# Written-out first attention with row moments taken inside it, and a routing stage normalized on two engines

## The chip, the core and the metric

The program runs on one core of a Trainium2 chip. A core has five engines that work side by side, each through its own queue of instructions in order: PE (TensorE, matmul and transposes), DVE (VectorE), ACT (ScalarE), POOL (GpSimd) and SP (SyncE, which here only issues DMA). They are ordered among one another by semaphores alone. The metric is the device time of one execution in microseconds, as the median of several runs. Before the change it is 2719.99 us, the median of three runs (2716.86 to 2720.1).

## What is computed

Two layers over a graph of 2708 nodes with 256 features. Layer 0 is a graph attention with four heads, followed by a mixture of experts; layer 1 is a masked attention with four heads, followed by 30 steps of a small feed-forward network. The change touches the end of layer 0's attention and the start of its mixture of experts:

```python
x = x + _L0_gnn_ref(_layernorm(x, axis=-1), adj, ...)          # graph attention
x = x + _L0_ffn_ref((_layernorm(x, axis=-1))[None], ...)[0]    # mixture of experts

# in _L0_gnn_ref, for each head
logits = f1[:, None, :] + f2[:, :, None]
w = jax.nn.leaky_relu(logits, NEG_SLOPE)
masked = w * adj_mat
neg = jnp.where(adj_mat != 0.0, masked, -jnp.inf)
e = jnp.exp(neg - m); attn = e / denom
out = jnp.einsum('hnm,hmo->hno', attn, support)

# in _L0_ffn_ref: 16 experts, 2 chosen
gate_logits = x @ gate_w + gate_b
topk_vals, topk_idx = jax.lax.top_k(gate_logits, K)
topk_w = jax.nn.softmax(topk_vals, axis=-1)
```

The layer norm between the two needs the mean and the variance of every row of x after the attention. These are the "row moments" of the title.

## The kernel before, in words

The 2708 rows lie in 22 tiles of 128 partitions (the last tile overlaps the one before), taken as 11 pairs (`NPAIR`). x stays in `X` for the whole kernel. Every stage is a `Phase` with a block of instructions per engine and a barrier of all engines at its end (the line of the barrier is L55 or L58).

*Layer 0's attention* (`layer0_attention`, tiles named `a_`). The work is a sequence of 88 units, one for each tile and head. For a unit, PE makes the logits in three chunks (L717, L719), DVE adds and applies the leaky part per chunk (`leaky`, L626), multiplies by the mask with a running maximum (`mask`, L635) and negates the maximum (L638); ACT takes the exponential (L571); PE transposes the weights in 22 squares (`turn`, L732), ACT copies them out of PSUM (L526), and PE multiplies them by the values (`weighted`, 44 matmuls a unit, L747). After two heads ACT copies the sums, PE turns them back (L755) and DVE scales and adds them to X (`finish`, L658). The stages of a unit are spread over the steps of later units. `over_units` (L431) writes the order: the first pair and the last pair are written out, and the nine between are a loop of three rounds whose body holds three pairs, because the buffers go round by three (`LB`):

```python
    pair(0, 0)
    with eng.Fori(0, (NPAIR - 2) // LB) as m:
        for r in range(LB):
            pair(m * LB + (r + 1), r + 1)
    pair(NPAIR - 1, NPAIR - 1)
```

PE, DVE and ACT each run this loop. Some waits of ACT and DVE stand on a `nop` of their own. POOL prepares the mask tiles, and SP loads the adjacency rows.

*Routing* (`moe_route`, tiles named `m_`). DVE takes `bn_stats` of each of the 22 tiles (L142) and folds them into moments in four batches (`row_moments`, L94 to L101); POOL, after its constants, computes the inverse deviation of a batch (`inverse_deviation`, L108 to L113, with a power at L111) and normalizes tile by tile into `XF` (`standard_rows`, L118). PE transposes a tile (L1484), ACT copies it (L1540), PE multiplies by the gate (L1492) and DVE adds the bias into the logits (L1553). PE alternates between the transposes of one tile and the product of the tile before. Then follows a chain, mostly on DVE, that picks two experts for each row and sorts the rows by expert (L1570 to L1661). Meanwhile SP issues the loads of the gate (L1408 to L1410, the last being beta), 32 loads of expert weights, and at last the stores of XF; POOL adds beta to X (L1472).

*Experts* (`moe_experts`). POOL gathers the sorted rows tile by tile (L1705), PE transposes them (L1732) and multiplies (L1742, L1752); DVE stages the weights of a tile's expert (L1783), copies the transposed rows (L1785) and adds the second bias (L1793). SP loads two biases at the start (L1694, and 2 MB for the second, L1695). DVE waits for that second bias after it has staged two tiles and before it stages the third.

## Time and profile before

| | us |
|---|---|
| median of three runs | 2719.99 |
| the profiled execution | 2717.6 |
| its span | 2715.9 |
| mean granted clock of PE, share of full | 0.952 |
| busy: PE, DVE, ACT, POOL | 2481.9, 2011.5, 1614.1, 1426.9 |
| layer 0's attention in the timeline | about 74 to 773 |
| routing | 773.8 to 851.4 |
| experts, from the first gather | 853.1 |

A row of the timeline gives the start, the duration, the engine, the line of the kernel, the operation, what it writes and reads, how many in a row (xN), and in brackets how long the engine was idle before it and what released it. "issue" means that nothing which the profile shows was waited for. PEld is the loading of weights, which overlaps PE. An engine with a q at its end (POOLq) is its sequencer.

### The profile page before, as it was taken

The numbers are of one execution on the slowest core, as the hardware profiler recorded it, in microseconds if no ns is written. First come the engines' busy times: TensorE is split into PE (matmuls) and PEld (weight loads), VectorE is DVE, ScalarE is ACT, GpSimd is POOL, SyncE is SP. The second block draws the span as 40 slices with busy tenths as digits, with TensorE's granted clock in tenths as the row PEclk, the third lists the DMA queues.
The fourth block names the chain that finished last, engine by engine and source line by source line (L and its number), as shares of the span: only waits on it lengthen the run. The fifth ranks groups of instructions, "written<-read, shape, count | busy, mean of one in ns | idle before, by whom it ended". The sixth has DMA issues, their size and how long they took to land. (4 is left out here: it accounts for less than half of the span.)

```text
span 2715.9 us, 59651 instructions
## 1 busy us (share of the span) xinstructions
PE 2481.9 (91%) x20186; PEld 2029.7 (75%) x20187; DVE 2011.5 (74%) x4258; ACT 1614.1 (59%) x3050; POOL 1426.9 (53%) x1747
## 2 busy tenths in 40 slices
PE   6799999999975999097999999999689999999999
PEld 5377777777764998075777777777578888888888
DVE  5899989899945443787777777777667777777776
ACT  1577777777730332244666666666467777777775
POOL 6366666666451554432111122111388888888886
PEclk9799999999976999598999999999899999999999
DMA  2011111111054222301111111110000000000001
GB/s 99 21 43 49 56 43 43 43 63 43 22 197 148 70 72 62 126 16 35 55 41 41 41 41 41 45 58 21 7 1 0 0 0 0 0 0 0 0 0 41
DMA packets 43885, 114.26 MB, mean 42 GB/s; under 512 B 5621, under 2 KB 29918, under 8 KB 37982
## 3 DMA queue, kind: packets, MB, share of 16 engines
q1 hardware_dynamic: 38174, 97.16, 10.2%
q0 software_dynamic: 5568, 15.21, 1.8%
q8 instruction: 87, 1.43, 0.2%
q14 instruction: 56, 0.46, 0.1%
HBM read 99.21 MB, written 13.15 MB: 41 GB/s over the span
## 5 line engine op out<-in xcount | busy, mean ns | idle before, releaser
L2145 PE MATMUL f_pm<-f_wl,f_yt 128*128 128x256 f32 x2640 | 625.6, 380 | 0.0
L2145 PEld LDWEIGHTS f_pm<-f_wl,f_yt 128*128 128x128 f32 x2640 | 477.2, 191 | 51.6
L1089 POOL TENSOR_TENSOR ADJ<-ADJ,a_off 128x2708 f32<-128x2708 f32 x22 | 131.2, 5962 | 543.1 <-DVE ADJ L1168 543.1
L118 POOL TENSOR_SCALAR f_yy<-f_th,f_rs 128x255 f32<-128x255 f32 x660 | 367.5, 573 | 21.8 <-POOL f_rs L113 21.8
L526 ACT COPY a_wt<-a_tp 128x512 f32<-128x512 f32 x528 | 256.9, 566 | 155.3 <-PE a_tp L732 155.3
L1995 DVE SCALAR_TENSOR_TENSOR f_gg<-f_th,f_pm 128x512 f32<-128x512 f32 x319 | 219.0, 687 | 171.4 <-ACT f_th L2089 170.3
L549 POOL TENSOR_SCALAR a_off<-ADJ 128x677 bf16<-128x677 f32 x84 | 278.3, 3334 | 78.3 <-DMA ADJ<-in_adj 63.7
L626 DVE SCALAR_TENSOR_TENSOR a_lg<-a_f1s,F2S,a_fo 128x1024 f32<-128x1024 f32 (+1 forms) x264 | 294.5, 1152 | 30.8 <-issue 17.1
L1148 DVE CUSTOM_DVE_ANT_0 a_sc<-a_qk,ADJ 128x1024 f32<-128x1024 f32 (+1 forms) x264 | 288.3, 1093 | 30.4 <-PE a_qk L1246 30.4
L2089 ACT ACTIVATE f_th<-f_pm 128x512 f32<-128x512 f32 x319 | 190.5, 597 | 199.7 <-PE f_pm L2145 199.7
L1112 ACT ACTIVATE a_sc<-a_sc,a_mx 128x1024 f32<-128x1024 f32 (+1 forms) x264 | 277.7, 1052 | 45.3 <-DVE a_mx L1153 45.3
L1063 ACT COPY a_wt<-a_tp 128x512 f32<-128x512 f32 x264 | 154.2, 584 | 236.2 <-PE a_tp L1268 235.5
L635 DVE CUSTOM_DVE_ANT_0 a_lg<-a_lg,ADJ 128x2708 f32<-128x2708 f32 x88 | 262.0, 2977 | 7.4 <-issue 0.7
L1268 PE MATMUL a_tp<-ident,a_sc 128*128 128x128 f32 x1936 | 261.7, 276 | 0.2
L732 PE MATMUL a_tp<-ident,a_lg 128*128 128x128 f32 x1936 | 247.4, 277 | 6.6 <-issue 6.0
L1268 PEld LDWEIGHTS a_tp<-ident,a_sc 128*128 128x128 f32 x1936 | 215.5, 141 | 42.1 <-issue 19.4
L2002 DVE BATCH_NORM_STATS2 f_st<-f_th 128x6 f32<-128x256 f32 x660 | 245.8, 414 | 0.0
L1289 PE MATMUL a_po<-a_wt,V 128*64 128x128 f32 x3872 | 240.3, 276 | 0.0
L1289 PEld LDWEIGHTS a_po<-a_wt,V 128*64 128x64 f32 x3872 | 208.7, 137 | 41.5 <-issue 36.3
L1063 DVE COPY a_wt<-a_tp 128x512 f32<-128x512 f32 (+1 forms) x264 | 158.3, 599 | 107.9 <-PE a_tp L1268 107.9
L747 PEld LDWEIGHTS a_po<-a_wt,V 128*64 128x64 f32 x3872 | 209.6, 137 | 37.1 <-issue 35.1
L732 PEld LDWEIGHTS a_tp<-ident,a_lg 128*128 128x128 f32 x1936 | 211.0, 142 | 33.2 <-issue 21.4
(295 smaller groups left out, 4572.0 us busy)
## 6 DMA issues: line engine op xcount, KB each, us to landing
ADJ<-in_adj SPq DMA_DIRECT2D x44, 1354.0 KB, 5.8
W<-in_L_ffn_w SPq DMA_DIRECT2D x32, 512.0 KB, 9.8
m_got<-YD SPq DMA_DIRECT2D x6, 768.0 KB, 10.4
out<-X SPq DMA_DIRECT2D x21, 128.0 KB
X<-in_x SPq DMA_DIRECT2D x3, 768.0 KB, 9.9
XD<-XF SPq DMA_DIRECT2D x3, 768.0 KB
m_b<-in_L_ffn_b SPq DMA_DIRECT2D x1, 2048.0 KB, 8.4
m_rows<-XD,SLOT POOLq DMA_INDIRECT x58, 2.8
```

The source lines that it names most:

```text
L118: return eng.tensor_scalar(out, x, rs[:, 0, bass.ds(t, 1)], rs[:, 1, bass.ds(t, 1)], ALU.mult, ALU.add)
L526: copy(wt[:, h // 2, h % 2, j:end, :], tp[:, BANKS[g], 0:(end - j) * P]).then_inc(copied[BANKS[g]], 1)
L549: pool.tensor_scalar(off[:, b, cols], adj[:, b, cols], 0.0, HUGE, ALU.is_equal, ALU.mult).then_inc(off_done[b], 1)
L626: dve.scalar_tensor_tensor(lg[:, unit.turn, c0:c0 + cn], f1s[:, h, c0:c0 + cn], F2S[:, bass.ds(i * 2 + b, 1), h], fo[:, s, 0:cn], ALU.add, ...
L635: dve.tensor_tensor_reduce(lg[:, unit.turn, :], lg[:, unit.turn, :], adj[:, b, :], 1.0, FLOOR, ALU.mult, ALU.max, mx[:, h, 0:1]).then_inc( ...
L732: mm = pe.transpose(tp[:, BANKS[g], (j - j0) * P:(j - j0 + 1) * P], lg[:, unit.turn, col:col + P], ident[:, :])
L1063: copy(wt[:, (hp * NC + c) % 2, s, j - c * CT:end - c * CT, :], tp[:, bank(group), 0:(end - j) * P]).then_inc(copied[bank(group)], 1)
L1112: act.activation(sc[:, h, c0:c0 + cn], sc[:, h, c0:c0 + cn], ACT.Exp, bias=mx[:, h, NC:NC + 1], accum_out=den[:, h, c:c + 1]).then_inc(exp ...
L1148: dve.tensor_tensor_reduce(sc[:, h, c0:c0 + cn], qk[:, s, 0:cn], adj[:, b, c0:c0 + cn], 1.0, -BIG, ALU.add, ALU.max, mx[:, h, c:c + 1]).th ...
L1268: mm = pe.transpose(tp[:, bank(group), (j - j0) * P:(j - j0 + 1) * P], sc[:, h, col:col + P], ident[:, :])
L1289: mm = pe.matmul(po[s * HD:(s + 1) * HD, 0:P], V[:, j, 2 * hp + s, 0:HD], wt[:, (hp * NC + c) % 2, s, j - c * CT, :], start=(j == 0), stop ...
L2145: mm = pe.matmul(out, yt[:, g, r, k, :], wl[:, k, :], start=(k == 0), stop=(k == KD - 1))
```

## The change

It has six parts.

1. `over_units` writes all 11 pairs out; the loop and its registers are gone on PE, DVE and ACT. The nops of ACT and DVE before the waits in the attention are gone as well (one in `rows_of`, one in `leaky`, one in `mask`).
2. DVE takes the row statistics of tiles 0 to 20 inside the attention (`row_stats`), at head 3 of the following tile, folds them into moments behind the last step, and POOL computes the inverse deviations of these 21 columns at its end, into the tensor `GW`, which now lives from there on and is called `scales` in the routing.
3. In the routing only the last tile's statistics are left. DVE normalizes the odd tiles and POOL the even ones; POOL's constants come after.
4. PE transposes and multiplies two tiles at a time; ACT copies 512 columns at once, and DVE adds the bias to two tiles at once. DVE's and ACT's loops there are written out.
5. A small tensor, `slot`, now lies in the space of `xt`.
6. In the experts SP waits for the first two gathers before it issues the load of the second bias.

The core of the diff:

```diff
-def inverse_deviation(pool, mom, rs, neg_half, s0, s1, chain, base):
+def inverse_deviation(pool, mom, rs, neg_half, s0, s1, chain, base, out=None):
 
 
     n = slice(s0, s1)
+    out = rs if out is None else out
     pool.tensor_scalar(rs[:, 2, n], mom[:, 1, n], EPS, None, ALU.add).then_inc(chain, 1)
     pool.tensor_scalar(rs[:, 3, n], mom[:, 0, n], -0.5, None, ALU.mult).then_inc(chain, 1)
     pool.wait_ge(chain, base + 1)
-    pool.tensor_tensor(rs[:, 0, n], rs[:, 2, n], neg_half[:, n], ALU.pow).then_inc(chain, 1)
+    pool.tensor_tensor(out[:, 0, n], rs[:, 2, n], neg_half[:, n], ALU.pow).then_inc(chain, 1)
     pool.wait_ge(chain, base + 3)
-    return pool.tensor_tensor(rs[:, 1, n], rs[:, 3, n], rs[:, 0, n], ALU.mult)
+    return pool.tensor_tensor(out[:, 1, n], rs[:, 3, n], out[:, 0, n], ALU.mult)
...
         for b in range(2):
             for h in range(H):
                 step(Unit(i, b, h, number * 2 * H + b * H + h))
-    pair(0, 0)
-    with eng.Fori(0, (NPAIR - 2) // LB) as m:
-        for r in range(LB):
-            pair(m * LB + (r + 1), r + 1)
-    pair(NPAIR - 1, NPAIR - 1)
+    for i in range(NPAIR):
+        pair(i, i)
...
             with pool.Fori(1, NPAIR) as i:
                 for b in range(2):
                     tile(i, b)
+            pool.wait_ge(x_moments, 1)
+            inverse_deviation(pool, mom, rs, neg_half, 0, NT - 1, x_pchain, 0, scales)
...
-                act.nop(nofuse=True)
...
-                dve.nop(nofuse=True)
...
+            def row_stats(unit):
+
+                i, b, h0 = unit
+                dve.wait_ge(heads_out, pairs(unit))
+                dve.bn_stats(st[:, i * 2 + b, :], X[:, i * 2 + b, :]).then_inc(x_stats, 1)
...
                     finish(unit.later(-4))
+                if unit[2] == H - 1 and unit.later(-H - 1):
+                    row_stats(unit.later(-H - 1))
                 if ahead:
...
             over_units(dve, step)
+            dve.wait_ge(x_stats, NT - 1)
+            row_moments(dve, st, mom, 0, NT - 1, x_folded, 0).then_inc(x_moments, 1)
             finish(last_unit(0))
             finish(last_unit(H - 2))
...
             for k, (a, end) in enumerate(BATCHES):
                 s0, s1 = 2 * a, min(2 * end, NT - 1)
-                sp.wait_ge(xf_done, 2 * end)
+                sp.wait_ge(xf_even, end)
+                sp.wait_ge(xf_odd, end)
                 sp.dma_start(keep["XD"][1 + P * s0:1 + P * s1, :].rearrange("(t p) d -> p t d", p=P),
                              XF[:, s0:s1, :]).then_inc(stored, 16)
...
             pool.memset(zero[:, :], 0.0).then_inc(zero_ok, 1)
+            for t in range(0, NT, 2):
+                standard_rows(pool, XF[:, t:t + 1, :], X[:, t:t + 1, :], scales, t).then_inc(xf_even, 1)
+                if t == 0:
+                    pool.wait_ge(moments, 1)
+                    inverse_deviation(pool, mom, rs, neg_half, 0, 1, pchain, 0, scales[:, :, NT - 1:NT]).then_inc(inv, 1)
             pool.memset(ones[:, :], 1.0).then_inc(ones_ok, 1)
...
-            for t in range(NT):
-                slot_deviation(pool, t, mom, rs, neg_half, moments, pchain, inv)
-                standard_rows(pool, XF[:, t:t + 1, :], X[:, t:t + 1, :], rs, t).then_inc(xf_done, 1)
-
             pool.wait_ge(w_in, 48)
-            pool.wait_ge(xf_done, NT)
+            pool.wait_ge(xf_even, NPAIR)
+            pool.wait_ge(xf_odd, NPAIR)
...
+            def turn(i):
+
+                pe.wait_ge(xf_even, i + 1)
+                pe.wait_ge(xf_odd, i + 1)
+                if i >= 2:
+                    pe.wait_ge(xt_done[i % 2], i // 2)
+                for r in range(2):
+                    for k in range(KD):
+                        mm = pe.transpose(pt[:, i % 2, (r * KD + k) * P:(r * KD + k + 1) * P],
+                                          XF[:, 2 * i + r, k * P:(k + 1) * P], ident[:, :])
+                mm.then_inc(turned[i % 2], 1)
+
+            def product(i):
+
+                pe.wait_ge(xt_done[i % 2], i // 2 + 1)
+                if i >= 2:
+                    pe.wait_ge(lg_done[i % 2], i // 2)
+                for r in range(2):
+                    for k in range(KD):
+                        mm = pe.matmul(pg[:, i % 2, r * E:(r + 1) * E], xt[:, i % 2, r, k, :], gw[:, k, :],
+                                       start=(k == 0), stop=(k == KD - 1))
+                mm.then_inc(g_mm[i % 2], 1)
+            turn(0)
             for i in range(NPAIR):
-                turn(i, 1)
-                product(i, 0)
                 if i < NPAIR - 1:
-                    turn(i + 1, 0)
-                product(i, 1)
+                    turn(i + 1)
+                product(i)
...
-            with act.Fori(0, NPAIR) as i:
-                for b in range(2):
-                    act.wait_ge(turned[b], i + 1)
-                    act.copy(xt[:, b, :, :], pt[:, b, 0:D]).then_inc(xt_done[b], 1)
+            for i in range(NPAIR):
+                act.wait_ge(turned[i % 2], i // 2 + 1)
+                act.copy(xt[:, i % 2, :, :, :], pt[:, i % 2, :]).then_inc(xt_done[i % 2], 1)
...
-            slot_moments(dve, X, st, mom, stats, folded, moments)
+            dve.bn_stats(st[:, 0, :], X[:, NT - 1, :]).then_inc(stats, 1)
+            standard_rows(dve, XF[:, 1:2, :], X[:, 1:2, :], scales, 1).then_inc(xf_odd, 1)
+            dve.wait_ge(stats, 1)
+            row_moments(dve, st, mom, 0, 1, folded, 0).then_inc(moments, 1)
+            for t in range(3, NT, 2):
+                if t == NT - 1:
+                    dve.wait_ge(inv, 1)
+                standard_rows(dve, XF[:, t:t + 1, :], X[:, t:t + 1, :], scales, t).then_inc(xf_odd, 1)
             dve.wait_ge(w_in, 48)
-            with dve.Fori(0, NPAIR) as i:
-                for b in range(2):
-                    dve.wait_ge(g_mm[b], i + 1)
-                    dve.tensor_tensor(lg[:, 0, bass.ds(i * 2 + b, 1), :], pg[:, b:b + 1, 0:E],
-                                      gb[:, :].rearrange("p (a e) -> p a e", a=1), ALU.add).then_inc(lg_done[b], 1)
+            for i in range(NPAIR):
+                dve.wait_ge(g_mm[i % 2], i // 2 + 1)
+                dve.tensor_tensor(lg[:, 0, 2 * i:2 * i + 2, :],
+                                  pg[:, i % 2, 0:2 * E].rearrange("p (r e) -> p r e", r=2),
+                                  gb[:, :].rearrange("p (a e) -> p a e", a=1).to_broadcast([P, 2, E]),
+                                  ALU.add).then_inc(lg_done[i % 2], 1)
             for b in range(2):
-                dve.wait_ge(lg_done[b], NPAIR)
+                dve.wait_ge(lg_done[b], (NPAIR + 1 - b) // 2)
...
             sp.dma_start(b1n, io["L0_ffn_b1"].rearrange("e (f p) -> (e f) p", p=P)).then_inc(b_in, 16)
+            sp.wait_ge(rows_in[0], 16)
+            sp.wait_ge(rows_in[1], 16)
             sp.dma_start(b2[:, :, :].rearrange("p e d -> p (e d)"),
                          bcast_rows(io["L0_ffn_b2"].rearrange("e d -> (e d)"), P)).then_inc(b2_in, 16)
```

On DVE in the attention a step reads as follows before, at the end of the loop's body and behind it (`a_lg` are the logits, `a_mx` the maximum, `a_rec` the reciprocals of the sums):

```order
L626 SCALAR_TENSOR_TENSOR a_lg<-a_f1s,F2S,a_fo 128x660
L633 REGISTER_ALU
L635 ISA a_lg,a_mx<-a_lg,ADJ 128x2708
L635 ISA a_mx 128x1
L638 TENSOR_SCALAR a_mx<-a_mx 128x1
L644 TENSOR_SCALAR a_rec<-a_den 128x2
L648 RECIPROCAL a_rec<-a_rec 128x2
L438 REGISTER_ALU
L438 COMPARE_AND_BRANCH
L626 SCALAR_TENSOR_TENSOR a_lg<-a_f1s,F2S,a_fo 128x1024 x2
```

and after the change, at head 3 of a tile:

```order
L629 SCALAR_TENSOR_TENSOR a_lg<-a_f1s,F2S,a_fo 128x1024 x2
L629 SCALAR_TENSOR_TENSOR a_lg<-a_f1s,F2S,a_fo 128x660
L668 BN_STATS a_st<-X 128x6
L637 ISA a_lg,a_mx<-a_lg,ADJ 128x2708
L637 ISA a_mx 128x1
L640 TENSOR_SCALAR a_mx<-a_mx 128x1
L646 TENSOR_SCALAR a_rec<-a_den 128x2
L650 RECIPROCAL a_rec<-a_rec 128x2
```

The branch and the register operations are gone, and the statistics (`a_st`) stand between the last chunk and the mask.

On DVE at the start of the routing, before (the first batch; three more follow it, then the adds):

```order
L142 REGISTER_ALU
L142 BN_STATS m_st<-X 128x6
L141 REGISTER_ALU
L141 COMPARE_AND_BRANCH
L94 TENSOR_TENSOR m_mom<-m_st 128x6
L95 TENSOR_TENSOR m_mom<-m_st 128x6
L96 TENSOR_TENSOR m_mom<-m_st 128x6
L98 SCALAR_TENSOR_TENSOR m_mom<-m_mom 128x6
L101 SCALAR_TENSOR_TENSOR m_mom<-m_mom 128x6
```

and after, up to the adds of the logits' bias:

```order
L1567 BN_STATS m_st<-X 128x6
L119 TENSOR_SCALAR XF<-X,GW 128x256
L94 TENSOR_TENSOR m_mom<-m_st 128x1
L95 TENSOR_TENSOR m_mom<-m_st 128x1
L96 TENSOR_TENSOR m_mom<-m_st 128x1
L98 SCALAR_TENSOR_TENSOR m_mom<-m_mom 128x1
L101 SCALAR_TENSOR_TENSOR m_mom<-m_mom 128x1
L119 TENSOR_SCALAR XF<-X,GW 128x256 x10
L1578 TENSOR_TENSOR m_lg<-m_pg,m_gb 128x32 x11
```

21 of 22 statistics and their moments have left, eleven normalizing operations have come from POOL, and 22 adds have become 11.

On PE in the routing, before, from its start:

```order
L1484 MATMUL m_pt<-ident,XF 128x128 x4
L1492 MATMUL m_pg<-m_gw,m_xt 128x16 x2
L1484 MATMUL m_pt<-ident,XF 128x128 x2
L1492 MATMUL m_pg<-m_gw,m_xt 128x16 x2
L1484 MATMUL m_pt<-ident,XF 128x128 x2
```

and after:

```order
L1502 MATMUL m_pt<-ident,XF 128x128 x8
L1513 MATMUL m_pg<-m_gw,m_xt 128x16 x4
L1502 MATMUL m_pt<-ident,XF 128x128 x4
L1513 MATMUL m_pg<-m_gw,m_xt 128x16 x4
L1502 MATMUL m_pt<-ident,XF 128x128 x4
```

The same matmuls, in groups of four; a product is executed as two halves, so the timeline shows twice as many rows of it.

## Rows read from the trace of the kernel before

**Rows 1.** Busy time by stretch: from:to, length, five engines, clock, DMA share, GB/s.

```profile
187.00:217.00 30.00, 30.00 (x323) 23.73 (x320) 27.84 (x33) 23.08 (x38) 19.70 (x9) 1.00 0.13 48
347.00:350.50 3.50, 2.73 (x13) 2.68 (x14) 2.47 (x2) 1.17 (x2) 1.17 (x1) 0.51 0.03 7
...
789.30:812.60 23.30, 22.98 (x116) 22.88 (x116) 3.48 (x20) 6.71 (x18) 22.33 (x38) 0.50 1.08 367
...
860.70:865.90 5.20, 5.05 (x22) 4.51 (x23) 1.70 (x4) 0.00 (x1) 1.97 (x2) 0.50 0.18 52
865.90:869.50 3.60, 3.60 (x27) 3.39 (x26) 1.11 (x2) 2.29 (x8) 0.94 (x1) 1.00 0.00 0
```

**Rows 2.** Waits of PE, 122 to 757 us: total us, times, longest.

```profile
PE a_tp L732 <- issue: 6.0, 2, 3.2
```

**Rows 3.** Timeline of PE in the attention: start, us, line, operation, [idle before <-releaser].

```profile
341.99 2.62 PE L747 MATMUL a_po<-a_wt,V 128*64 128x128 f32 x44
347.77 2.82 PE L732 MATMUL a_tp<-ident,a_lg 128*128 128x128 f32 x12 [3.15 <-issue]
...
354.02 2.62 PE L747 MATMUL a_po<-a_wt,V 128*64 128x128 f32 x44
...
738.41 2.62 PE L747 MATMUL a_po<-a_wt,V 128*64 128x128 f32 x44
...
745.92 1.31 PE L747 MATMUL a_po<-a_wt,V 128*64 128x128 f32 x20
```

**Rows 4.** Timeline of DVE and ACT late in the attention.

```profile
739.84 0.15 DVE L638 TENSOR_SCALAR a_mx<-a_mx 128x1 f32<-128x1 f32 x1
...
743.25 2.58 ACT L571 ACTIVATE a_lg<-a_lg,a_mx 128x2708 f32<-128x2708 f32 x1
```

**Rows 5.** Operations of the kinds moved; ns min/median/max or mean.

```profile
L142 DVE BATCH_NORM_STATS2 m_st<-X x22: 426/427/428, 774.2 to 787.0; - x22
...
L118 POOL TENSOR_SCALAR XF<-X,m_rs x22: 551/556/587, 780.2 to 798.3; 128x256 f32<-128x256 f32 x22
...
L111 POOL TENSOR_TENSOR m_rs<-m_rs,neg_half x4: 1039/1354/1366, 778.4 to 795.3; 128x6 f32<-128x6 f32 x3, 128x4 f32<-128x4 f32 x1
...
L2055 DVE TENSOR_SCALAR f_wl<-f_wt,f_lnwb 128x256 f32<-128x256 f32 x2 | 0.6, 345 | 0.0
```

**Rows 6.** Timeline of the routing.

```profile
780.85 0.29 PEld L1484 LDWEIGHTS m_pt<-ident,XF 128*128 128x128 f32 x2 [8.64 <-DMA m_beta<-in_L_ffn_beta]
780.88 1.14 PE L1484 MATMUL m_pt<-ident,XF 128*128 128x128 f32 x4 [8.48 <-POOL XF L118]
...
789.31 1.01 PE L1492 MATMUL m_pg<-m_gw,m_xt 128*128 128x16 f32 x4 [4.59 <-DVE m_lg L1553]
790.15 0.67 PE L1484 MATMUL m_pt<-ident,XF 128*128 128x128 f32 x2
790.62 0.87 PE L1492 MATMUL m_pg<-m_gw,m_xt 128*128 128x16 f32 x4
791.33 0.67 PE L1484 MATMUL m_pt<-ident,XF 128*128 128x128 f32 x2
...
812.45 0.17 DVE L1553 TENSOR_TENSOR m_lg<-m_pg,m_gb 128x16 f32 x1 [0.68 <-PE m_pg L1492]
```

**Rows 7.** The experts' start: timeline, then two DMA issues (us to landing last).

```profile
853.09 1.23 POOL L1705 DMA_INDIRECT m_rows<-XD,SLOT  x1 [38.80 <-POOLq L58]
...
854.62 0.95 POOL L1705 DMA_INDIRECT m_rows<-XD,SLOT  x1 [0.30 <-issue]
...
860.69 0.69 PE L1732 MATMUL m_pt<-ident,m_rows 128*128 128x128 f32 x2 [5.83 <-DMA m_rows<-XD,SLOT]
...
869.46 1.95 PE L1742 MATMUL m_p<-m_xt,m_w 128*128 128x128 f32 x16
...
m_b<-in_L_ffn_b SPq DMA_DIRECT2D x1, 2048.0 KB, 8.4
...
m_rows<-XD,SLOT POOLq DMA_INDIRECT x58, 2.8
```

More of the change, by code:

```diff
@@ L455, in layer0_attention @@
 def layer0_attention(nc, io, keep):
-    X, V, F2S, FP, ROWS, SEL, HSEL, IDB, ident, adj, adj_in = (
-        keep[n] for n in ("X", "V", "F2S", "FP", "ROWS", "SEL", "HSEL", "IDB", "ident", "ADJ0", "adj_in"))
+    X, V, F2S, FP, ROWS, SEL, HSEL, IDB, ident, neg_half, adj, adj_in = (
+        keep[n] for n in ("X", "V", "F2S", "FP", "ROWS", "SEL", "HSEL", "IDB", "ident", "neg_half", "ADJ0", "adj_in"))
+    scales = keep["GW"]
     with Phase(nc, "a0") as ph:
+        st = ph.sb("st", [P, NT, 6])
+        mom = ph.sb("mom", [P, 5, NT])
+        rs = ph.sb("rs", [P, 4, NT])
         off = ph.sb("off", [P, 2, N], BF16)
@@ L1340, in moe_route @@
     X, ident, neg_half = (keep[n] for n in ("X", "ident", "neg_half"))
-    XF, SLOT, GW, TE = (moe[n] for n in ("XF", "SLOT", "GW", "TE"))
+    XF, SLOT, TE = (moe[n] for n in ("XF", "SLOT", "TE"))
+    GW = scales = keep["GW"]
     NA = TOPK * NT
@@ L1476, in _ @@
             pe.wait_ge(w_in, 48)
-            def turn(i, b):
-                t = i * 2 + b
-                pe.wait_ge(xf_done, t + 1)
-                if some(i):
-                    pe.wait_ge(xt_done[b], i)
-                for k in range(KD):
-                    mm = pe.transpose(pt[:, b, k * P:(k + 1) * P], XF[:, t, k * P:(k + 1) * P], ident[:, :])
-                mm.then_inc(turned[b], 1)
-            def product(i, b):
-                pe.wait_ge(xt_done[b], i + 1)
-                if some(i):
-                    pe.wait_ge(lg_done[b], i)
-                for k in range(KD):
-                    mm = pe.matmul(pg[:, b, 0:E], xt[:, b, k, :], gw[:, k, :], start=(k == 0), stop=(k == KD - 1))
-                mm.then_inc(g_mm[b], 1)
-            turn(0, 0)
+            def turn(i):
[18 more added lines that the diff above has]
+            turn(0)
             for i in range(NPAIR):
-                turn(i, 1)
-                product(i, 0)
                 if i < NPAIR - 1:
-                    turn(i + 1, 0)
-                product(i, 1)
+                    turn(i + 1)
+                product(i)
             pe.wait_ge(consts, 12 + 4 * TOPK)
@@ L2196, in build @@
         adj_in = [whole.enter_context(nc.semaphore(f"adj_in{k}")) for k in range(4)]
+        early = whole.enter_context(ExitStack())
+        keep.update(buffers(early, GW=([P, TOPK, NT],)))
         with ExitStack() as part:
```

25 lines of the change are left out of this document (13 added, 12 removed).

## The prediction

> **What bounds the kernel now.** I read the page first: its slices say which stretches have a busy PE at full clock. The attention of layer 0 is one of them, the routing that follows is not. Then busy time by stretch, for what each stage is limited by; the waits of PE inside the attention; timelines of PE at the places where the change touches it; and last the routing and the start of the experts, engine by engine. The second layer is left alone by the change; I take its time as it is.
>
> In the attention PE is the bound: 30.00 of 30.00 us busy at full clock, DVE 27.84 [rows 1]. Its waits from 122 us on are headed by two stops of 6.0 us in all that have no releaser but "issue" [rows 2]. They are the two places where the loop of three pairs jumps back (11 pairs, two of them written out, leave three rounds). In the routing PE stands for 4.59 us, waiting for the bias add on DVE, which is behind all the row statistics in DVE's order, and then works without a pause at half clock to the last logits, 22.98 of 23.30 us busy [rows 1, 6]. In the experts PE starts 7.6 us after the first gather is issued [rows 7].
>
> **The change, part by part.**
>
> *The attention without loops.* A unit is seen on PE from one start of the 44 weighting matmuls to the next. A unit that jumps nowhere takes 745.92 - 738.41 = 7.51 us; the one with the jump takes 354.02 - 341.99 = 12.03 [rows 3]. The difference is 4.52: the stop itself, 3.15, and the rest because the clock afterwards is granted at 0.51, the level of 1.2 GHz, for 3.50 us [rows 1]. The second jump is one of the same wait group; two at 4.52 are **9.0 us**, all on the path since PE has no slack. The 7.51 is from the last pairs, which are already written out, so straight code as such is no slower than the loop; its code must be fetched once more in either case, as the loop's rounds are. Bounds: 6.0 (the stops alone) to 9.0.
>
> Here a rule speaks against so much. The Trainium skill, "Advanced Engine Details and Errata", Control Flow Timing, gives a compare-and-branch about 108 ns; by it two jumps would be worth some 0.2 us, and the whole sum below would be 7.5 instead of 16.3. The row with its 3.15 us decides against it.
>
> *Removed nops* on ACT and DVE: no instruction that PE waits for; PE's order is the bound. Nothing, and nothing if that cover goes, since fewer instructions cannot be later.
>
> *Row statistics in the attention.* 21 of 0.43 us [rows 5] go to DVE, one a tile, between the third chunk and the mask at head 3. Behind them are the mask and the negated maximum, for which ACT's exponential waits. The exponential began 743.25 - 739.99 = 3.3 us after its maximum was there [rows 4], so 0.43 us is covered, and DVE has 2.2 us free in 30 to catch up [rows 1]. If that cover went, the price would be 21 x 0.43 = 9.0 (a rival below). The moments (five small operations) and the inverse deviation stand behind the last tiles; the power costs 1.04 us for 4 columns and 1.35 for 6 [rows 5], so 1.04 + 17 x 0.157 = 3.7 for 21. DVE and POOL are idle there while PE does its last weighting. Cost 0; at worst, if the phase ended on POOL, 1 to 2 us.
>
> *The routing.* Two things held its PE: the start at 780.88, for the first normalized rows, and the stop of 4.59 [rows 6]. PE also needs three small loads, and its first weight load, at 780.85, has the last of them, beta, as its releaser [rows 6]. So rows that are normalized sooner bring nothing at the start. The stop goes: DVE has now one statistic (0.43), five small operations and eleven normalizing ones of at most 0.345 by the nearest row [rows 5], 5 to 6 us altogether, and is through when beta lands. POOL normalizes one tile, computes the last tile's inverse deviation (with its power of about a microsecond), and then normalizes ten more at 0.556 [rows 5]. If DVE and POOL kept each other out completely, a pair of tiles would still come every 0.556 + 0.345 = 0.90 us, and PE takes 2.3 us a pair. So PE's own pace decides.
>
> One tile takes 791.33 - 790.15 = 1.18 us [rows 6], 22 take 26.0: from 780.85 to 806.85. Before, the last add started at 812.45, a tenth behind its matmuls; at the same pace that is a gain of 5.5. By pairs the pace may be worse. Two transposes (0.67) and the product halves of one tile (0.87) overlap in the mixture by 0.67 + 0.87 - 1.18 = 0.36 a tile [rows 6], and by pairs there are half as many seams. If all of that is lost, 11 x 0.36 = 4.0 go back and 1.5 is left. But four transposes in a row took 1.14 [rows 6], 0.20 less than twice 0.67, which leaves a loss of 0.16 a pair, 1.8 altogether, and a gain of 3.7. Bounds 1.5 to 5.5; I take **4.7**, about halfway from 3.7 to 5.5, since neither row is of this order of work. The eleven adds fewer on DVE lie in its waiting. POOL's constants move behind its normalizing, which ends some 10 us into the phase; DVE and PE want them behind the logits, more than 20 us later, and the additions of beta after them are wanted by nobody in this phase. SP's stores of the normalized rows stand behind 32 weight loads in its queue as before, so they do not move. The chain on DVE behind the logits is unchanged and moves as a whole.
>
> *The experts' start.* SP now waits for two gathers before the 2 MB bias load. The first gathers, beside that load, kept PE until 860.69; alone a gather takes 2.8 [rows 7], so rows are there at 853.09 + 2.8 = 855.9 and 854.62 + 2.8 = 857.4: 4.8 sooner. But DVE waits for the bias before it stages the third tile's weights: load issued 857.5, landed 8.4 later [rows 7] at 865.9, staged at 866.6. The matmuls of the third tile began at 869.46, so at most 2.9 come through. Bounds 0 (the load runs late by as much) to 4.8 (the load is quicker when alone); I take **2.6**: the 2.9 less a little for the third and fourth gather, which now run beside the load. Nothing is queued on SP behind its wait; on DVE the staging of all further tiles is, and PE waits for that.
>
> Sum: 9.0 + 4.7 + 2.6 = 16.3. The profiled execution took 2717.6 us (span 2715.9 and 1.7 around it): 2701.3. It stands 2.4 below the median of the runs shown, 2719.99, which would give 2703.7. I say 2702.5, between the two. A difference under 0.2% (5.4 us) is what a measurement of this kernel cannot tell from none.
>
> **The rivals.**
>
> *A. The clock rises within the routing.* PE now works 26 us there without a stop. At the experts' start full clock came 5.2 us after PE began [rows 1]. The same here would put it at 786.1, and the remaining 20.8 us of half-clock work would take 10.4: 2702.5 - 10.4 = 2692. Against it: with the same mixture of transposes and thin products PE was busy 22.98 of 23.30 us and stayed at 0.50 [rows 1]. The Trainium skill, "TensorE: Matmul & The Clock Gate", Part 1, has an engine that stays busy given the full clock, which is this rival; its Part 4 excepts transposes. The trace so far sides with the exception. 7%.
>
> *B. The statistics are in the way.* DVE is 93% busy in the attention; if each 0.43 delays a mask that PE does need, 9.0 go: 2711.5. For it: DVE, ACT and PE form a ring three units deep. Against it: 3.3 us of slack [rows 4]. 8%.
>
> *C. Slower: straight code is fetched late.* Suppose the stop at the jump is instructions that are not there yet, and PE runs out of them in straight code too, once at each of the nine pairs that were looped. Each stop costs 4.5: 40.7 in all, minus the gain of 16.3: 24.4 slower, 2743. From four stops (16.3/4.5 = 3.6) nothing is left, from five it is slower by over 0.2%. Against it: within the loop's rounds and in the last pair, straight code as well, no such stop is in the waits [rows 2]. The Trainium skill, "Runtime: NRT & Kernel Launch", Instruction fetch mechanics, also has straight code loaded ahead and only a jump out of the loaded stretch wait. 3%.
>
> *D. The gains do not come through.* PE's stop at the jump turns out to be a wait for something else (ACT or DVE jump too), and reappears at fewer places; or the bias load holds the experts by more than the gather gives. With both stops left and nothing from the experts, 4.7 remains: 2714, no difference. 5%.
>
> **How the numbers follow.** The forecast has 77%, its own range from 2717.6 - 9.0 - 5.5 - 4.8 = 2698.3 to 2720.0 - 6.0 - 1.5 - 0 = 2712.5. A, B, C, D have 7, 8, 3 and 5. The range 2692 to 2712 takes in A's and B's values and leaves out C, D and what lies beyond in A and B, with some of the forecast's ends: no more than 2 in 10. Faster by over 0.2%: forecast, A and B, 0.91 with a little off for what I overlook: 0.90. Within 0.2%: 0.06. Slower: 0.04.
>
> **What would show it.** Each step has its sign in the new profile: no wait of PE on issue in the attention and all units at 7.4 to 7.5; the phase of routing begins near 764.8; first transposes of the routing some 7 us after that, no wait on the add, and pairs at 2.35 to 2.5 us, at clock 0.50; first expert transposes about 3 us after the first gather, then a wait of DVE for the bias load. Wrong would be: a new idle time of DVE or ACT in the attention that ends at the statistics, a wait of PE on XF, the routing's clock at 1.00, or a third tile's matmuls not sooner than 16 us after the first gather.

## The result, and the profile after

The kernel after takes 2704.67 us, median of 5 runs (2703.6 to 2707.88), against 2718.63 of 5 runs of the kernel before: ratio 0.9951, 95% interval 0.9941 to 0.9962. That is 14.0 us faster by the medians, and 0.49% by the ratio. The forecast was 2702.5. The profiled execution took 2703.6 us, with a span of 2701.8, against 2717.6 and 2715.9 of before.

First busy time by stretch in the kernel after, in the columns of [rows 1]:

```profile
187.00:217.00 30.00, 30.00 (x322) 23.74 (x320) 27.77 (x34) 23.19 (x39) 19.82 (x9) 1.00 0.13 48
345.00:352.00 7.00, 7.00 (x75) 5.60 (x76) 6.61 (x9) 5.61 (x9) 3.80 (x3) 1.00 0.01 4
...
772.00:799.50 27.50, 27.45 (x132) 27.12 (x132) 1.92 (x11) 6.45 (x11) 20.88 (x55) 0.50 1.08 369
```

PE is the bound of the attention as before. At 345 to 352 us, where the first jump of before cost a stop and a stretch at clock 0.51, it is now busy throughout at 1.00. The routing is still at 0.50. The waits of PE in the attention (132 to 757 us) are down to one line; the two stops on issue of [rows 2] are gone:

```profile
PE a_po L759 <- DVE X L660: 0.6, 1, 0.6
```

The timeline of after (start, us, engine, line, operation, idle before and its releaser) answers to [rows 3, 5, 6, 7]:

```profile
126.27 2.62 PE L759 MATMUL a_po<-a_wt,V 128*64 128x128 f32 x44
...
342.27 2.62 PE L759 MATMUL a_po<-a_wt,V 128*64 128x128 f32 x44
...
349.77 2.40 PE L759 MATMUL a_po<-a_wt,V 128*64 128x128 f32 x40
...
763.33 0.33 PE L767 MATMUL a_po<-ident,a_ot 128*128 128x128 f32 x1 [0.36 <-ACT a_ot L584]
...
766.56 3.40 DVE L119 TENSOR_SCALAR XF<-X,GW 128x256 f32<-128x256 f32 x10
...
768.63 6.07 POOL L119 TENSOR_SCALAR XF<-X,GW 128x256 f32<-128x256 f32 x10
...
771.99 1.97 PE L1502 MATMUL m_pt<-ident,XF 128*128 128x128 f32 x8 [8.33 <-DMA m_beta<-in_L_ffn_beta]
...
775.51 1.09 PE L1502 MATMUL m_pt<-ident,XF 128*128 128x128 f32 x4
...
777.96 1.09 PE L1502 MATMUL m_pt<-ident,XF 128*128 128x128 f32 x4
...
799.49 0.19 DVE L1578 TENSOR_TENSOR m_lg<-m_pg,m_gb 128x32 f32<-128x32 f32 x1 [1.52 <-PE m_pg L1513]
...
840.19 1.25 POOL L1734 DMA_INDIRECT m_rows<-XD,SLOT  x1 [47.24 <-POOLq L58]
...
843.23 0.69 PE L1761 MATMUL m_pt<-ident,m_rows 128*128 128x128 f32 x2 [0.75 <-DMA m_rows<-XD,SLOT]
...
853.06 0.69 DVE L1812 COPY m_w<-W 128x1024 f32 x1 [7.08 <-DMA m_b<-in_L_ffn_b]
...
854.38 1.95 PE L1771 MATMUL m_p<-m_xt,m_w 128*128 128x128 f32 x16
```

- Attention: the unit at 342 takes 349.77 - 342.27 = 7.50 us, not 12.03. From the first weighting to PE's last turn back it is 763.33 - 126.27 = 637.06 us. The same two lines of before stand at 126.02 and 772.07, 646.05 apart. So 9.0 went.
- Routing: from that turn back to the last add it is now 799.49 - 763.33 = 36.16. Before it was 812.45 - 772.07 = 40.38, so 4.2 went. A pair takes 777.96 - 775.51 = 2.45.
- Experts: from the first gather to the third tile's matmuls it is 854.38 - 840.19 = 14.19. Before it was 869.46 - 853.09 = 16.37 [rows 7], so 2.2 went.

These three make 15.4. PE's first weighting is 0.25 later (126.02 against 126.27), and PE's last product in the experts starts 15.08 sooner (1076.48 against 1061.40). From there to the end of the span it is 1.0 longer than before (1640.4 against 1639.4), so 14.1 are left of the 15.1. PE's first long wait there is 1.1 shorter (71.79 against 70.66), and one at the feed-forward's start is 1.2 longer (10.4 against 11.6, for the bias sums of DVE); the other 0.9 lies in small pieces that no run here separates. Nothing in the code of this stage was changed, and why the wait of 11.6 is longer is open. In before and the three kernels with only loops written out (below) it is 10.0 to 10.4; in after and four of its variants it is 11.6 to 11.8, in the other variants less than 11, though all of them keep the attention's part of the change.

### The profile page after: what moved, and what is told of

Same layout as the page of the kernel before. It is cut to its first block and busy times, and to the rows that moved or that the text cites. A ratio compares the mean times of both kernels' runs of the same rounds, so it can differ in the third digit from the quotient of the medians.

```text
span 2701.8 us, 58198 instructions
## 1 busy us (share of the span) xinstructions
PE 2479.9 (92%) x20186; PEld 2029.4 (75%) x20187; DVE 2001.9 (74%) x4248; ACT 1611.9 (60%) x3039; POOL 1419.9 (53%) x1728
## 5 line engine op out<-in xcount | busy, mean ns | idle before, releaser
L552 POOL TENSOR_SCALAR a_off<-ADJ 128x677 bf16<-128x677 f32 x84 | 284.3, 3407 | 76.2 <-DMA ADJ<-in_adj 61.8
L576 ACT ACTIVATE a_lg<-a_lg,a_mx 128x2708 f32<-128x2708 f32 x88 | 226.5, 2574 | 11.9 <-DVE a_mx L640 11.4
```

What stands on the lines that cost most here:

```text
L552: pool.tensor_scalar(off[:, b, cols], adj[:, b, cols], 0.0, HUGE, ALU.is_equal, ALU.mult).then_inc(off_done[b], 1)
```

## Experiments: the loops

**All three engines without loops, the rest as before.** The edit to the kernel before:

```diff
-    pair(0, 0)
-    with eng.Fori(0, (NPAIR - 2) // LB) as m:
-        ...
-    pair(NPAIR - 1, NPAIR - 1)
+    for i in range(NPAIR):
+        pair(i, i)
```

> The kernel before with the attention's order written out on PE, DVE and ACT, and nothing else of the change (the nops stay). Theory T, the jumps of the loop are what the attention loses: both stops of PE go, every unit takes 7.4 or 7.5 us, the attention ends about 9.0 us sooner and the span is near 2707. Rival, the cost of a compare-and-branch alone (0.1 us a jump): no change that can be measured, the stops of about 3 us reappear at the same units. Rival C, straight code is fetched late: new stops of 3 us or so elsewhere.

Measured: 2709.68 us (2708.59 to 2711.16, 5 runs) against 2719.25, ratio 0.9964 (0.995 to 0.9978). The timeline of PE:

```profile
129.81 1.42 PE L744 MATMUL a_po<-a_wt,V 128*64 128x128 f32 x22
...
766.75 0.33 PE L752 MATMUL a_po<-ident,a_ot 128*128 128x128 f32 x1 [0.37 <-ACT a_ot L576]
```

From the first weighting to PE's last turn back (called the attention proper from here on) it takes 636.94, 9.1 less than before, which is the whole of what after shows. No wait on issue is left on PE. Its first weighting comes 3.8 us later than in before, in a start-up phase in which the clock goes up and down, so in this execution the attention ends only 5.3 sooner and the span is 6.4 shorter; the medians differ by 9.6. Why the start is late is open. The kernel below with the loops of ACT and DVE written out shares it (129.79), the one with PE's does not (126.53). After has the nops removed and the statistics added as well, and its attention proper is 637.06: together these two cost or give 0.1.

**PE alone without loops**, and **DVE and ACT alone** (the loop stays on PE). The same branch, chosen by an argument: `over_units(pe, step, True)` in the first, `over_units(act, step, True)` and `over_units(dve, step, True)` in the second.

> The kernel before with the order written out on PE alone; DVE and ACT keep their loops. Theory T1, PE's own jump is the whole stop: span near 2707, 9 us under before, both units at 7.5 us. Theory T2, every engine's jump holds up that engine by some 3.4 us and PE sees those of the others as far as its lead over DVE is short (about 1 us for the logits): 2 to 3 us are left at each of the two jumps, now as a wait on DVE or ACT and not on issue; span 2710 to 2713.

> The mirror of the former: order written out on DVE and ACT, PE keeps its loop. T1: as before, 2716, both units of 12.0 us, stops on issue. T2: nearly as before as well, since PE's own stop of 3 us hides theirs; perhaps half a microsecond less per jump. If this one is 9 us faster, the stop put down to issue on PE was DVE's or ACT's.

Measured, one run each: 2714.64 and 2720.9, against 2719.25 of before. With PE written out, first its wait in the attention, then what DVE and PE do at the place of the first jump:

```profile
PE a_fo L721 <- DVE a_lg L630: 5.4, 2, 2.8
```

```profile
348.03 2.47 DVE L630 SCALAR_TENSOR_TENSOR a_lg<-a_f1s,F2S,a_fo 128x1024 f32<-128x1024 f32 x2 [3.31 <-issue]
...
349.37 0.46 PE L721 MATMUL a_fo<-a_off,IDB 128*128 128x512 bf16 x2 [2.78 <-DVE a_lg L630]
```

With DVE and ACT written out:

```profile
PE a_tp L736 <- issue: 5.9, 2, 3.0
```

PE and DVE each have a stop of their own of about 3 us where they jump: PE up to 3.0, DVE 3.31, both on issue. In before they lie beside each other: PE's ends at 347.77 [rows 3] and DVE's at 347.66:

```profile
347.66 2.47 DVE L626 SCALAR_TENSOR_TENSOR a_lg<-a_f1s,F2S,a_fo 128x1024 f32<-128x1024 f32 x2 [3.45 <-issue]
```

On ACT, which jumps as well, no wait on issue shows in any of these kernels; its idle time there is put down to PE. Taking away one stop leaves the other on the path: the attention proper is 770.93 - 126.53 = 644.4 and 774.47 - 129.79 = 644.7 us, 1.6 and 1.4 less than before, where both together give 9.1. So most of the cost falls only when PE's jump and DVE's are both gone. (The times of the two kernels, of one run each, say less than these rows: the second has the late start.)

The queues that carry instructions give a hint at what the engines stop for. Between 132 and 757 us they moved (queue, packets, MB, share), in before, then queue 8 with PE written out (queue 14 has its 34 as before), then queue 14 with DVE and ACT written out (queue 8 has its 58):

```profile
q8 instruction: 58, 0.95, 0.7%
q14 instruction: 34, 0.28, 0.2%
...
q8 instruction: 52, 0.85, 0.5%
...
q14 instruction: 20, 0.16, 0.1%
```

Queue 8 loses 6 blocks when PE's loop goes and none when the others' go; queue 14 loses 14 when DVE's and ACT's go and none when PE's goes. So a jump costs extra loads of instructions. At the first one a block of queue 8 starts between 344.25 and 344.50 and takes 1.5 us; PE's idle time begins at 344.62. This speaks for stops that wait for code. It is not shown that the loads are what ends them, since the profile names no releaser. Straight code is loaded too, 52 blocks of it on queue 8, without a wait of PE on issue.

## Experiments: the row statistics

**Four statistics a tile, then two.** The kernel after, with three further statistics of the same rows that nothing reads (in the second kernel one, `range(1)`):

```diff
+                for _ in range(3):
+                    dve.bn_stats(more[:, i * 2 + b, _, :], X[:, i * 2 + b, :])
                 dve.bn_stats(st[:, i * 2 + b, :], X[:, i * 2 + b, :]).then_inc(x_stats, 1)
```

> The changed kernel with four row statistics per tile in the attention instead of one (three more of 0.43 us at the same place, written to a tensor that nobody reads; 66 of 0.43 more would be 28 us if all of it were on the path). My theory, that DVE has about 2.2 us free in the 30 of a tile and the exponential comes 3.3 us behind its maximum: 1.7 us a tile fits, units stay at 7.4 and 7.5, span within 1 us of the changed kernel's 2701.8. Rival B, each statistic in front of the mask is in PE's way: up to 27 us more, 2729.

> The kernel after, with each tile's row statistics taken twice in the attention (0.42 us more on VectorE, once a tile). Four statistics lengthened one unit of every tile from 7.4 to 8.39 us, for 1.25 us more of work. If VectorE has no cover left behind the one statistic, 0.42 us comes out at 0.4 us a tile and some 8 us in all; if cover remains, of about 0.3 us as the run with four says (0.98 lost of 1.25), the second one costs 0.1 us a tile and 0 to 3 us in all. The prediction's 2.2 us free in 30 would say nothing at all.

Measured: 2720.01 with four (one run), 2704.51 with two (2702.25 to 2706.33, 4 runs), 2704.67 with one. The waits of PE and its timeline with four:

```profile
PE a_fo L732 <- DVE a_lg L630: 13.5, 19, 0.7
```

```profile
194.84 2.62 PE L762 MATMUL a_po<-a_wt,V 128*64 128x128 f32 x44
...
199.63 0.46 PE L732 MATMUL a_fo<-a_off,IDB 128*128 128x512 bf16 x2 [0.71 <-DVE a_lg L630]
...
203.22 0.98 PE L762 MATMUL a_po<-a_wt,V 128*64 128x128 f32 x14
```

and with two:

```profile
194.04 2.62 PE L762 MATMUL a_po<-a_wt,V 128*64 128x128 f32 x44
201.55 2.62 PE L762 MATMUL a_po<-a_wt,V 128*64 128x128 f32 x44
```

With two the unit is 7.51 us, as with one, and the attention proper 764.02 - 127.05 = 636.97: not a tenth is lost. With four the same unit takes 203.22 - 194.84 = 8.38, 0.87 more for 1.25 us of statistics, once in nearly every tile, and the attention proper 653.98, 16.9 more. So between 0.42 and 1.25 us beyond the one statistic the cover ends, near 0.4 by the 0.87 that comes through. It does not end at the exponential, whose slack I had read, but at DVE's next chunk: PE waits with its additive chunks (L732), 19 times, for DVE's leaky sum (L630), which has to read the PSUM bank before PE may write it again. And the 2.2 us that DVE has free in 30 are no slack of that size, as the 0.87 lost shows: DVE works in a fixed order against PE, and only idle time that lies between the statistics and what PE waits for can take up their time.

## Experiments: the routing

**Logits by single tiles again**, on PE, ACT and DVE; moments and normalizing as in after. The core on PE:

```diff
-            turn(0)
-            for i in range(NPAIR):
-                if i < NPAIR - 1:
-                    turn(i + 1)
-                product(i)
+            turn(0, 0)
+            for i in range(NPAIR):
+                turn(i, 1)
+                product(i, 0)
+                if i < NPAIR - 1:
+                    turn(i + 1, 0)
+                product(i, 1)
```

> The kernel after, with the logits by single tiles again on TensorE, ScalarE and VectorE, while the normalizing stays on two engines. The prediction charges the pairs with a loss of pace of 0.16 us a pair against the 1.18 us a tile of before (2.36 a pair), and after shows 2.45 a pair. If that holds, single tiles are 0.09 us a pair faster in the loop and some 0.5 us faster at its fill and its drain: the last add ends 1 to 1.5 us sooner, and the span is that much shorter. The rival that the pairs spare semaphore turns and therefore time says 1 us or more longer: the tile's pace was set by the hand-over between TensorE and ScalarE, not by TensorE's own work, and returns to over 1.25 us a tile.

Measured: 2701.56 us (2700.44 to 2702.55, 4 runs) against 2718.94. The timeline:

```profile
773.03 1.12 PE L1499 MATMUL m_pt<-ident,XF 128*128 128x128 f32 x4 [8.25 <-DMA m_beta<-in_L_ffn_beta]
...
775.06 0.67 PE L1499 MATMUL m_pt<-ident,XF 128*128 128x128 f32 x2
...
776.23 0.67 PE L1499 MATMUL m_pt<-ident,XF 128*128 128x128 f32 x2
...
799.58 0.17 DVE L1575 TENSOR_TENSOR m_lg<-m_pg,m_gb 128x16 f32<-128x16 f32 x1 [0.68 <-PE m_pg L1507]
```

A tile takes 1.17, two 2.34 against 2.45 by pairs. From the first transposes to the last add it is 26.55 against 799.49 - 771.99 = 27.50: the pairs cost 0.95 us. No stop comes back without them. The median is 3.1 below after's, more than the routing gives: 1.3 of it is the wait in the second layer's feed-forward, 10.3 here and 11.6 in after. That wait is 10.4 in before and in the kernel with two statistics, 11.8 in the one with the bias load first. Where a difference of medians is of this size, I go by the stage's own rows.

**GpSimd normalizes all 22 tiles**, DVE none:

```diff
-            for t in range(0, NT, 2):
-                standard_rows(pool, ...).then_inc(xf_even, 1)
+            for t in range(NT):
+                ...
+                standard_rows(pool, ...).then_inc((xf_even, xf_odd)[t % 2], 1)
```

> The kernel after, with all 22 tiles of the routing normalized by GpSimd alone, as before the change; the moments stay in the attention and the logits stay by pairs. In the trace of after the first transposes are held by the load of the beta until 771.99 and a pair takes 2.45 us, while GpSimd at 0.56 to 0.61 us a tile has two tiles ready by about 769.5 and a pair every 1.2 us. So by the prediction's reading (VectorE's statistics made the stop of 4.59, not the normalizing) the second engine is worth nothing: the span stays within 0.5 us, and no stop stands between the logits. The rival that the second engine is what took the stop away says a stop of 1 us or more comes back in the first pairs, and 1 to 4 us on the span.

Measured: 2701.81 us (2700.99 to 2702.66, 4 runs) against 2719.03. The timeline:

```profile
767.39 11.34 POOL L119 TENSOR_SCALAR XF<-X,GW 128x256 f32<-128x256 f32 x21
...
771.55 1.97 PE L1504 MATMUL m_pt<-ident,XF 128*128 128x128 f32 x8 [8.38 <-DMA m_beta<-in_L_ffn_beta]
...
799.06 0.19 DVE L1575 TENSOR_TENSOR m_lg<-m_pg,m_gb 128x32 f32<-128x32 f32 x1 [1.51 <-PE m_pg L1515]
```

From the first transposes to the last add: 27.51, as in after, with no stop between. The second engine is worth nothing in the routing. The median is 2.9 below after's; the profiled execution places 0.5 of that ahead of the first weighting and 1.3 in the two long waits of the second layer's feed-forward (10.8 and 12.7 against 11.6 and 13.2), neither of which this edit touches. Neither the pairs nor the second engine took away the 4.59 of [rows 6], then. What is left is that DVE has no statistics in front of its adds, and the rows of before say the same. From 774.18 on DVE was at its statistics and moments, and its first add followed the last of the moments at once, at 789.00; PE went on at 789.31:

```profile
789.00 0.24 DVE L1553 TENSOR_TENSOR m_lg<-m_pg,m_gb 128x16 f32 x2
```

Statistics put back alone were not tried.

**A semaphore for each of the three loads**, so that PE waits for the gate's weight alone:

```diff
-            sp.dma_start(gw[:, :, :], ...).then_inc(w_in, 16)
-            sp.dma_start(gb[:, :], ...).then_inc(w_in, 16)
+            sp.dma_start(gw[:, :, :], ...).then_inc(gw_in, 16)
+            sp.dma_start(gb[:, :], ...).then_inc(gb_in, 16)
...
-            pe.wait_ge(w_in, 48)
+            pe.wait_ge(gw_in, 16)
```

> The kernel after, with the routing's three loads on semaphores of their own: TensorE waits for the gate's weight alone, VectorE for the gate's bias, GpSimd for the first load. The prediction says that TensorE's first transpose is held by the last of the three loads. If so, the first transpose starts 2 to 5 us sooner (its data are normalized about 1.5 us behind the phase's start), and all of it arrives at the last logits and in the span: 2 to 4.5 us shorter. If instead the gate's weight lands as late as the beta, as all three are issued within a microsecond of each other, the gain is below 1 us.

Measured: 2702.0 us (2701.73 to 2703.12, 4 runs) against 2718.94. The timeline:

```profile
766.87 0.66 PE L1502 MATMUL m_pt<-ident,XF 128*128 128x128 f32 x4 [3.17 <-DMA m_gw<-in_L_ffn_gate_w]
769.92 1.12 PE L1502 MATMUL m_pt<-ident,XF 128*128 128x128 f32 x4 [2.40 <-POOL XF L119]
...
796.38 0.19 DVE L1578 TENSOR_TENSOR m_lg<-m_pg,m_gb 128x32 f32<-128x32 f32 x1 [1.51 <-PE m_pg L1513]
```

PE starts 5.1 sooner, then stands 2.40 for GpSimd, which computes the last tile's inverse deviation before its second tile, and takes 1.19 for that tile instead of 0.55 (more on this below); the last add comes 3.1 sooner. The beta, which PE never reads, held the start, as the prediction said.

**The same with extra work on PE**: ten multiplications of the identity by itself ahead of the first transposes, three ahead of each pair's products. Nothing reads their result.

```diff
+            for _ in range(10):
+                pe.matmul(pr[:, 0, 0:P], ident[:, :], ident[:, :], start=True, stop=True)
             pe.wait_ge(gw_in, 16)
```

> The kernel with the loads on semaphores of their own, and TensorE given extra multiplications of the identity by itself, which nothing reads: ten ahead of the first transposes and three ahead of each pair's products. It asks whether the half clock of the routing comes from TensorE's gaps and thin work (rival A of the prediction). If this work keeps the clock at 1.00, a pair takes 1.7 us or less instead of 2.45, and the last logits end 6 to 9 us sooner than in the run with the semaphores alone. If the clock stays at 0.50, the three extra multiplications cost up to 1 us a pair, and the run is 5 to 11 us slower than that one. I lean to the second, since the clock in before rose only where the experts' dense multiplications began.

Measured: seven runs in two groups, four at 2716.4 to 2717.31 and three at 2698.9, 2699.08 and 2700.34 (ratio over all 0.996, 0.9937 to 0.9983). The mean granted clock of whole runs is 0.952 to 0.953 in the first group and 0.959 to 0.960 in the second. The profile is of the first. Busy time by stretch:

```profile
768.00:770.00 2.00, 0.84 (x8) 0.84 (x9) 1.25 (x4) 0.14 (x1) 2.00 (x3) 1.00 0.32 116
770.00:772.00 2.00, 2.00 (x15) 2.00 (x14) 0.01 (x1) 0.44 (x1) 2.00 (x5) 0.63 1.01 366
...
770.00:808.00 38.00, 38.00 (x188) 38.00 (x186) 1.92 (x10) 5.72 (x10) 22.20 (x57) 0.51 1.07 368
```

The clock is full at the first transposes (766.76) and falls to half between 770 and 772. Ahead of the fall PE had stood 1.80 us, until 769.16, for GpSimd's second tile; from 770 on it is busy without a gap. A pair then takes 3.73 us by the starts of its transposes, 1.28 more than without the extra work. An estimate from these numbers: a run that is about 17 us shorter did some 35 us of its half-clock work at full clock, and that alone would raise the mean from 0.9525 to about 0.959, what the second group shows. The 38 us from 770 to 808 would be long enough for it, and nothing else was edited. But no execution of the second group was profiled, so it is not shown that the full clock was granted there, and whether the half clock of the routing can be avoided stays open. This is no version to keep, as most of its runs lose 14 against the same kernel without the extra work.

## Experiments: the experts' start, and a version of the best parts

**The bias load no longer waits for the gathers** (SP's two waits on `rows_in` removed from after), and **DVE waits for the bias later** (ahead of the first output, behind the staging of the third tile).

> The kernel after, with one thing undone: the queue of the b2 load no longer waits for the gathers of the two first tiles' rows. By the prediction's term for the experts' start, the first turn then waits for rows that arrive late again (about 7.6 us behind the gather instead of 3.0), the rest of the start is late by what the change gained there, and the span is 2.2 us longer (from 1.8 to 2.9, since the term measured 2.2 between the two kernels), all of it present at the end of the experts and most of it at the end of the kernel. The rival that the experts' start gained nothing by itself, and that its 2.2 us come from the gathers being issued at another moment, says no difference within 0.5 us.

> The kernel after, with VectorE's wait for b2 moved behind its staging of the third tile, so that it stands right ahead of the first output that reads b2. If b2's late landing (8.4 us after its issue) is what holds the third tile, as the trace of after says (VectorE idle 7.08 us up to 853.06), the third tile is staged when its rows are there, about 2 us sooner or more, TensorE's first long wait in the experts shrinks by 1 to 3 us, and the span falls by 1 to 2.5 us. If the first output is bound by b2 in any case (it needs b2 and then the next turn's bank), the gain is below 0.5 us.

Measured: 2706.82 us (2705.89 to 2707.65) and 2704.83 us (2704.0 to 2706.62), 4 runs each, against 2718.94. The timeline of the first:

```profile
840.92 1.25 POOL L1732 DMA_INDIRECT m_rows<-XD,SLOT  x1 [47.24 <-POOLq L58]
...
848.80 0.69 PE L1759 MATMUL m_pt<-ident,m_rows 128*128 128x128 f32 x2 [5.84 <-DMA m_rows<-XD,SLOT]
...
857.58 1.95 PE L1769 MATMUL m_p<-m_xt,m_w 128*128 128x128 f32 x16
```

and of the second:

```profile
840.89 1.25 POOL L1734 DMA_INDIRECT m_rows<-XD,SLOT  x1 [46.85 <-POOLq L58]
...
848.82 0.69 DVE L1812 COPY m_w<-W 128x1024 f32 x1 [2.09 <-PE m_p L1771]
...
852.20 0.44 PE L1761 MATMUL m_pt<-ident,m_rows 128*128 128x128 f32 x2 [1.74 <-DMA m_rows<-XD,SLOT]
...
855.00 1.95 PE L1771 MATMUL m_p<-m_xt,m_w 128*128 128x128 f32 x16
```

With the bias load first, rows are there 7.9 us after the gather instead of 3.0, and the third tile starts 857.58 - 840.92 = 16.66 after it instead of 14.19: 2.5, and the median is 2.15 longer. With DVE's wait moved, the third tile's weights are staged 7.93 us after the first gather instead of 12.87, yet its matmuls start 14.11 after it, no sooner. Its rows, gathered now beside the bias load, land so that PE waits for them until 852.20. In both kernels the matmuls start 1.83 us after PE's products for an earlier tile (852.55 in after, 853.17 here), which in PE's order stand behind the transposes of these rows. In after, DVE was through with the staging and the copy behind the bias at 854.09, 0.3 ahead of the matmuls. So two waits of almost one length lie there, the rows' a little longer, and removing the one I had named gives nothing.

**Separate semaphores, single tiles, and GpSimd's inverse deviation of the last tile behind its fifth tile** (`if t == 8`).

> The version that the runs so far point to: the kernel after with the three loads on semaphores of their own (worth 3.1 us, of which a wait of 2.40 for GpSimd's second tile was left), GpSimd's row moments of the last tile moved behind its fifth tile so that this wait goes too, and the logits by single tiles (1.0 us). The first transposes start at about 767, the tiles follow each other every 1.17 us without a stop, the last add ends 6 us sooner than in after: 2698 to 2699.5 us. The rival says that GpSimd's pace (0.61 us a tile of its own, so a pair in 1.2) or the gate's weight is late and only 4 us come: 2701.

Measured: 2698.5 us (2697.02 to 2699.44, 5 runs) against 2719.03: ratio 0.9925 (0.9911 to 0.9938), the fastest of all. The timeline:

```profile
767.21 1.11 PE L1499 MATMUL m_pt<-ident,XF 128*128 128x128 f32 x4 [3.45 <-DMA m_gw<-in_L_ffn_gate_w]
...
772.16 1.01 PE L1507 MATMUL m_pg<-m_gw,m_xt 128*128 128x16 f32 x4 [1.08 <-DVE m_lg L1575]
...
795.18 0.17 DVE L1575 TENSOR_TENSOR m_lg<-m_pg,m_gb 128x16 f32<-128x16 f32 x1 [0.68 <-PE m_pg L1507]
```

The last add comes 4.3 sooner than in after, not 6. One stop of 1.08 is left: PE waits for an add on DVE, in front of which stand DVE's normalizing operations. They run without a gap from 767.70 to 771.94, so DVE did not wait for the inverse deviation, which was there at 769.81. They start 1.1 later than in after and take 4.24 us instead of 3.40; GpSimd normalizes beside them for much of that time. The time is in the range that was expected, but its way there is not: 4.3 come from the routing, and of the rest of the 6.2 by which the median is shorter, 1.2 is again the second layer's wait (10.4 in the profile of this kernel).

## Why the prediction was right

- **Attention without loops, 9.0:** measured 9.0 in after and 9.1 with the loops written out alone. The prediction took the stop for PE's own. The kernel with PE alone written out shows that DVE's jump stops it too, and rival D's remark that another engine's jump could take its place would have come true had PE or DVE kept its loop. The rule on control flow in the Trainium skill ("Advanced Engine Details and Errata", Control Flow Timing), by which two jumps are worth 0.2, is too small by a factor of some 40 here. What agrees is the Trainium skill's "Runtime: NRT & Kernel Launch", Instruction fetch mechanics: a jump to code outside the loaded stretch must fetch it first, and straight code is loaded ahead. The counts of queues 8 and 14 above, 6 and 14 blocks fewer without the jumps, fit it. Rival C fell with that, since not one wait on issue is left on PE.
- **Row statistics, 0:** right, and in after the power of 21 columns took 3.73 us (POOL, L112) against 3.7. The reasons given were not good ones. The 3.3 us of slack at the exponential and the 2.2 free in 30 would both have allowed the 1.25 us more of four statistics, which cost 16.9. The true cover is about 0.4 beyond the one. Rival B had the right mechanism and began just outside the change.
- **Routing, 4.7:** measured 4.2. The start stayed with the beta's load, the stop went, a pair takes 2.45 (2.3 in its text, 2.35 to 2.5 in its signs). The pairs lose 0.95 in all; the prediction took 0.8, about halfway between 1.8 and nothing, and that it came so close is partly luck. The rest of the miss lies in the 22 x 1.18 = 26.0 us for all tiles: by single tiles it took 26.55.
- **Experts' start, 2.6:** measured 2.2, and 2.5 by undoing it. The wait of DVE for the bias is there (7.08), but it is not alone, as the moved wait shows: the third tile's rows, gathered beside the load, are as late. The prediction took a little off for these later gathers and did not see that their late rows would end last, by 0.3 us.
- **The sum:** 16.3 predicted, 15.4 in the stages, 14.1 in the spans and 14.0 in the medians. Between stages and spans lie the start-up (0.25) and what follows the experts (1.0). The prediction took the second layer as it is, which its code is; its time is not, and the wait at the feed-forward's start (1.2) is the largest single loss.
- **Rival A:** the routing stayed at 0.50, as the Trainium skill has it for transposes ("TensorE: Matmul & The Clock Gate", Part 4). 7% was fair. With multiplications added in the same place three of seven runs came out 17 us shorter than the other four, and 3 shorter than without them, so something of this rival may be had; where in these runs the clock was higher is not shown.

## What to carry to other kernels

A jump back over a long loop body, here six tiles of attention, can stop each engine that makes it for about 3 us. Where two engines stop at the same place, most of the cost falls only when both jumps are gone. The loops that are left in the kernel, with other bodies, show no such wait on PE from the experts on. Count from unit to unit on the bound engine, since the half clock behind the stop adds to it (4.5 in all for 3.15 here). Idle time of an engine is no measure of what can be put on it: double and quadruple the added operation and see where it comes through. Before an engine is blamed for a late start, look at what its semaphore counts: here a load that PE never read held it for 5 us.

## What was not expected of the hardware

- A stop at a jump was up to 3.2 us on PE and 3.45 on DVE: nearly the same on engines with different work, and it can hide behind another engine's.
- With the same extra work the same kernel ran at 2699 or at 2717 us and at mean granted clocks of 0.960 or 0.953: the clock that one kernel is granted can differ from run to run. Where in the run it differed is not shown.
- While DVE ran its ten normalizing operations back to back (766.56 to 769.96), GpSimd's one that began at 768.63 took 1.19 us. Its others, nearly all behind DVE's, took 0.55 to 0.58. Where it normalizes alone, all 22 took 0.548 to 0.560. Its tiles in after (ns, shortest/median/longest):

```profile
L119 POOL TENSOR_SCALAR XF<-X,GW x11: 548/556/1190, 765.4 to 774.1; 128x256 f32<-128x256 f32 x11
```

So the two engines do hold each other up when they normalize at the same time. Here it cost nothing, since PE was not waiting for rows yet; in the kernel with separate semaphores it is part of PE's wait of 2.40.
